# Three blocks of the first product in flight, and an even second product, in a mixture-of-experts loop

## What is computed

```python
a = jnp.einsum('th,eih->eti', hf, w1)
g = jnp.einsum('th,eih->eti', hf, w3)
eo = jnp.einsum('eti,ehi->eth', jax.nn.silu(a) * g, w2)
out = jnp.einsum('eth,te->th', eo, cw)
return hidden_states + out.reshape(B, S, H)
```

## Time and profile before

| | us |
|---|---|
| median of 3 runs (lowest to highest) | 2165.48 (2162.01 to 2167.72) |
| the profiled execution | 2174.44 |
| its span from first to last instruction | 2172.7 |
| TensorE matmul busy | 1881.4 |
| VectorE, ScalarE, GpSimd busy | 1453.2, 1220.9, 1219.0 |
| mean granted TensorE clock | 0.917 |

### The profile page before, as it was taken

How to read it: one execution, slowest core, us unless ns; L and a number is a source line. 1 busy time by engine, 2 the same in 40 slices (tenths; PEclk the granted TensorE clock), 3 DMA queues, 4 the chain that set the end, 5 groups by cost and what they waited for, 6 DMA issues and landing times. The chain is left out here.

```text
span 2172.7 us, 36357 instructions
## 1 busy us (share of the span) xinstructions
PE 1881.4 (87%) x12326; PEld 1352.7 (62%) x12326; DVE 1453.2 (67%) x2914; ACT 1220.9 (56%) x2305; POOL 1219.0 (56%) x989
## 2 busy tenths in 40 slices
PE   1898799999999999997994999925999999999996
PEld 0454355554454555553543988814889998899986
DVE  5477577777787877785762777844666666666663
ACT  0165566666666656674662554404666666666663
POOL 6443454545546445553324366642777777777775
PEclk8599899999999999997996999957999999999998
DMA  2655345555454566443503112126666666666662
GB/s 85 119 114 104 92 100 108 111 115 121 90 119 85 112 124 122 101 95 65 107 21 104 39 71 94 69 76 219 199 201 198 185 190 202 198 198 185 190 198 53
DMA packets 117005, 270.61 MB, mean 125 GB/s; under 512 B 15802, under 2 KB 49722, under 8 KB 116436
## 3 DMA queue, kind: packets, MB, share of 16 engines
q1 hardware_dynamic: 102516, 249.57, 43.5%
q0 software_dynamic: 14304, 18.72, 4.8%
HBM read 196.50 MB, written 71.73 MB: 123 GB/s over the span
## 5 line engine op out<-in xcount | busy, mean ns | idle before, releaser
L701 DVE TENSOR_REDUCE nraw<-ps 128x1 f32<-128x512 f32 x1024 | 649.2, 681 | 256.6 <-PE ps L848 254.8
L614 ACT ACTIVATE spare<-ps 128x512 f32<-128x512 f32 x1024 | 570.9, 602 | 394.7 <-PE ps L858 392.9
L1743 POOL TENSOR_TENSOR u_lo<-u_f,u_hi 128x256 fp32r<-128x256 f32 x273 | 343.6, 1268 | 164.6 <-ACT u_hi L1774 163.9
L1845 PE MATMUL ps_e<-x_hi,we_hi 128*128 128x256 f32 x1092 | 316.5, 290 | 9.0 <-DVE we_lo L1664 4.5
L848 PE MATMUL ps<-kst,qst 50*128 50x512 f32 x1024 | 290.8, 461 | 23.4 <-DVE nraw L701 17.2
L1845 PE MATMUL ps_e<-x_hi,we_lo 128*128 128x256 f32 x1092 | 305.5, 280 | 0.0
L1845 PE MATMUL ps_e<-x_lo,we_hi 128*128 128x256 f32 x1092 | 305.5, 280 | 0.0
L858 PEld LDWEIGHTS ps<-qst,kst 52*128 52x128 f32 x1024 | 106.6, 190 | 298.9 <-ACT spare L614 205.3
L858 PE MATMUL ps<-qst,kst 52*128 52x512 f32 x1024 | 281.8, 516 | 7.3 <-ACT spare L614 7.0
L870 PE MATMUL ps<-spare,vaug 128*32 128x512 f32 x2048 | 287.4, 635 | 0.0
L1704 DVE TENSOR_TENSOR u_f<-ps_e,silu 128x256 f32<-128x256 f32 x273 | 114.9, 421 | 235.2 <-PE ps_e L1845 133.9
(11 more groups left out here) (224 smaller groups left out, 3834.7 us busy)
## 6 DMA issues: line engine op xcount, KB each, us to landing
we_raw<-in_experts_w SPq DMA_DIRECT2D x117, 896.0 KB, 4.8
parts_kept<-parts SPq DMA_DIRECT2D x64, 512.0 KB, 3.3
kst<-parts_kept SPq DMA_DIRECT2D x192, 128.0 KB, 4.8
qst<-parts_kept SPq DMA_DIRECT2D x192, 128.0 KB, 7.2
x_raw<-xs SPq DMA_DIRECT2D x39, 259.0 KB, 2.8
x<-sum_tok SPq DMA_DIRECT2D x16, 512.0 KB, 2.6
x_tok<-x SPq DMA_DIRECT2D x16, 512.0 KB, 3.9
x_tok<-in_x SPq DMA_DIRECT2D x8, 512.0 KB, 4.5
```

The source lines that it names most:

```text
L614: act.activation(probs[:, e % 8], ps[:, score_bank(e, par)], ACT.Exp, scale=SCALE).then_inc(exp_made, 1)
L701: dve.tensor_reduce(nraw[:, g % 2, qt, half, i:i + 1], ps[:, max_bank(m, par)], AX.X, ALU.max, negate=True).then_inc(max_made, 1)
L1743: pool.tensor_tensor(u_lo[:, it], u_f[:, slot], u_hi[:, it].bitcast(F32), ALU.subtract).then_inc(ulo_made, 1)
L1845: ins = pe.matmul(ps[:, 2 * slot + c, 0:GR], left, right, start=m == 0, stop=m == len(terms) - 1)
```

## The change

- UPS = 3 slots for `silu` and `u_f`, and three PSUM banks for the first product: bank q % 3 for block q = 7n + it, with c = 0 in its first half and c = 1 in its second. `up` of q waits for `u_f` of q - 3, `u_f` of q for `u_lo` of q - 3. `silu` waits for both halves of its bank.
- LAG = 4: behind each `up` of block q stands `down` of block q - 4, the same in every place; four are left behind the loop.
- The sums of the second product have two pairs of banks by turns, and `eo_sb` two buffers: `put_out` waits for the adds of the step before the last, not the last.
- Both halves of the turned rows share bank 7. The turns stand in blocks 0 and 1, `x_hi` in blocks 1 and 3 and `x_lo` in block 4, both waiting for both turns. Before the loop both turns are issued without the wait for `x_lo` between them.
- `put_out` stands in block 5, the adds in block 5 (t = 0) and block 1 of the step after (t = 1). Behind the loop GpSimd issues the second add of step 37 and both of step 38.

```diff
@@ -60,6 +60,7 @@
 ROUTE_STEPS = 24
+UPS, LAG = 3, 4
 DX = D + 3
@@ -1607,11 +1608,11 @@
     x_lo = sb("x_lo", [P, 2, KD, GR], F32R)
-    silu = sb("silu", [P, 2, GR])
-    u_f = sb("u_f", [P, 2, GR])
+    silu = sb("silu", [P, UPS, GR])
+    u_f = sb("u_f", [P, UPS, GR])
     u_hi = sb("u_hi", [P, KI, GR], F32R)
     u_lo = sb("u_lo", [P, KI, GR], F32R)
-    eo = sb("eo_sb", [P, GT, D])
+    eo = sb("eo_sb", [P, 2, GT, D])
     x_in = [sem("x_in0"), sem("x_in1")]
@@ -1628,6 +1629,8 @@
     added = sem("added")
+
+    OUT_BANK, X_BANK = UPS, 7
 
@@ -1665,8 +1668,8 @@
             def lo_of_x(n, k, mt):
-                dve.wait_ge(xhi_made, n * 2 + mt + 1)
-                dve.scalar_tensor_tensor(x_lo[:, k, mt], ps[:, 7, 0:GR], rms_col[:, mt:mt + 1],
+                dve.wait_ge(xhi_made, n * 2 + 2)
+                dve.scalar_tensor_tensor(x_lo[:, k, mt], ps[:, X_BANK, mt * GR:(mt + 1) * GR], rms_col[:, mt:mt + 1],
                                          x_hi[:, k, mt].bitcast(F32), ALU.mult, ALU.subtract) \
@@ -1696,12 +1699,12 @@
                 for it in range(KI):
-                    slot = (k + it) % 2
-                    dve.wait_ge(silu_made, n * KI + it + 1)
-                    dve.wait_ge(up_mm, n * (2 * KI) + 2 * it + 2)
-                    if positive(n * KI + it - 1):
-                        dve.wait_ge(ulo_made, n * KI + it - 1)
-                    dve.tensor_tensor(u_f[:, slot], ps[:, 2 * slot + 1, 0:GR], silu[:, slot],
+                    q = n * KI + it
+                    dve.wait_ge(silu_made, q + 1)
+                    dve.wait_ge(up_mm, 2 * q + 2)
+                    if q >= UPS:
+                        dve.wait_ge(ulo_made, q - UPS + 1)
+                    dve.tensor_tensor(u_f[:, q % UPS], ps[:, q % UPS, GR:2 * GR], silu[:, q % UPS],
                                       ALU.mult).then_inc(u_made, 1)
@@ -1711,8 +1714,9 @@
                         lo_of_w(n + 1, 1 - k, it // 2)
-                    if it in (4, 6):
-                        lo_of_x(n + 1, 1 - k, (it - 4) // 2)
+                    if it == 4:
+                        for mt in range(KD):
+                            lo_of_x(n + 1, 1 - k, mt)
 
@@ -1731,23 +1735,26 @@
                 pool.indirect_dma_start(
-                    out=scratch["out"], in_=eo[:, t], in_offset=None,
+                    out=scratch["out"], in_=eo[:, n % 2, t], in_offset=None,
                     out_offset=bass.IndirectOffsetOnAxis(ap=targets[:, n % 3, t:t + 1], axis=0),
...
                 for it in range(KI):
-                    slot = (k + it) % 2
-                    pool.wait_ge(uhi_made, n * KI + it + 1)
-                    pool.tensor_tensor(u_lo[:, it], u_f[:, slot], u_hi[:, it].bitcast(F32),
+                    q = n * KI + it
+                    pool.wait_ge(uhi_made, q + 1)
+                    pool.tensor_tensor(u_lo[:, it], u_f[:, q % UPS], u_hi[:, it].bitcast(F32),
                                        ALU.subtract).then_inc(ulo_made, 1)
...
                         keep_rows(i, n, k)
-                    if n and it in (3, 6):
-                        add(n - 1, it // 6)
+                    if n >= 2 and it == 1:
+                        add(n - 2, 1)
+                    if n and it == 5:
+                        add(n - 1, 0)
 
             over_steps(pool, body)
+            add(STEPS - 2, 1)
             for t in range(GT):
@@ -1763,15 +1770,16 @@
             def hi_of_x(n, k, mt):
-                act.wait_ge(xt_mm, n * 2 + mt + 1)
-                act.activation(x_hi[:, k, mt], ps[:, 7, 0:GR], ACT.Copy, scale=rms_col[:, mt:mt + 1]) \
+                act.wait_ge(xt_mm, n * 2 + 2)
+                act.activation(x_hi[:, k, mt], ps[:, X_BANK, mt * GR:(mt + 1) * GR], ACT.Copy, scale=rms_col[:, mt:mt + 1]) \
                     .then_inc(xhi_made, 1)
...
                     act.wait_ge(down_kt, n * KI + it + 1 - KI)
-                act.activation(u_hi[:, it], u_f[:, (k + it) % 2], ACT.Copy).then_inc(uhi_made, 1)
+                act.activation(u_hi[:, it], u_f[:, (n * KI + it) % UPS], ACT.Copy) \
+                    .then_inc(uhi_made, 1)
 
@@ -1783,10 +1791,10 @@
                 act.wait_ge(share_made, n + 1)
-                if n:
-                    act.wait_ge(added, 16 * GT * n)
+                if n >= 2:
+                    act.wait_ge(added, 16 * GT * (n - 1))
                 for t in range(GT):
-                    act.activation(eo[:, t], ps[:, 4 + t, 0:D], ACT.Copy,
+                    act.activation(eo[:, k, t], ps[:, OUT_BANK + GT * k + t, 0:D], ACT.Copy,
                                    scale=shares[:, k, t:t + 1]).then_inc(eo_made, 1)
@@ -1797,22 +1805,22 @@
                 for it in range(KI):
-                    slot = (k + it) % 2
-                    act.wait_ge(up_mm, n * (2 * KI) + 2 * it + 1)
-                    if positive(n * KI + it - 1):
-                        act.wait_ge(u_made, n * KI + it - 1)
-                    act.activation(silu[:, slot], ps[:, 2 * slot, 0:GR], ACT.Silu) \
+                    q = n * KI + it
+                    act.wait_ge(up_mm, 2 * q + 2)
+                    if q >= UPS:
+                        act.wait_ge(u_made, q - UPS + 1)
+                    act.activation(silu[:, q % UPS], ps[:, q % UPS, 0:GR], ACT.Silu) \
                         .then_inc(silu_made, 1)
...
                         hi_of_u(n, k, it - 1)
-                    if it == 2 and n:
+                    if it == 5 and n:
                         put_out(n - 1, 1 - k)
...
                         hi_of_w(n + 1, 1 - k, it // 2)
-                    if it in (3, 6) and not last:
-                        hi_of_x(n + 1, 1 - k, it // 6)
+                    if it in (1, 3) and not last:
+                        hi_of_x(n + 1, 1 - k, it // 2)
                 hi_of_u(n, k, KI - 1)
@@ -1823,17 +1831,17 @@
                     pe.wait_ge(x_in[k], i * 16 + 16)
-                if positive(n * 2 + mt):
-                    pe.wait_ge(xlo_made, n * 2 + mt)
+                if n:
+                    pe.wait_ge(xlo_made, n * 2)
                 for t in range(GT):
-                    ins = pe.transpose(ps[:, 7, t * P:(t + 1) * P],
+                    ins = pe.transpose(ps[:, X_BANK, mt * GR + t * P:mt * GR + (t + 1) * P],
                                        x_raw[:, k, t, mt * P:(mt + 1) * P], ident[:, :])
...
             def up(n, k, it):
-                slot = (k + it) % 2
-                if positive(n * KI + it - 1):
-                    pe.wait_ge(u_made, n * KI + it - 1)
+                q = n * KI + it
+                if q >= UPS:
+                    pe.wait_ge(u_made, q - UPS + 1)
                 for c in range(2):
@@ -1842,15 +1850,15 @@
                     for m, (left, right) in enumerate(terms):
-                        ins = pe.matmul(ps[:, 2 * slot + c, 0:GR], left, right, start=m == 0,
+                        ins = pe.matmul(ps[:, q % UPS, c * GR:(c + 1) * GR], left, right, start=m == 0,
                                         stop=m == len(terms) - 1)
...
                     pe.wait_ge(wlo_made, n * 3 + 3)
-                    if positive(n):
-                        pe.wait_ge(eo_made, GT * n)
+                    if n >= 2:
+                        pe.wait_ge(eo_made, GT * (n - 1))
                 pe.wait_ge(ulo_made, n * KI + it + 1)
@@ -1858,7 +1866,7 @@
                     for m, (left, right) in enumerate(terms):
-                        ins = pe.matmul(ps[:, 4 + t, 0:D], left, right, start=it == 0 and m == 0,
+                        ins = pe.matmul(ps[:, OUT_BANK + GT * k + t, 0:D], left, right, start=it == 0 and m == 0,
                                         stop=it == KI - 1 and m == len(terms) - 1)
@@ -1870,17 +1878,14 @@
                     up(n, k, it)
-
-                    if it >= 3:
-                        down(n, k, it - 3)
-                    elif it < 2 and not (isinstance(n, int) and n == 0):
-                        down(n - 1, 1 - k, KI - 2 + it)
-                    if it in (2, 5) and not last:
-                        turn_rows(i + k, n + 1, 1 - k, it // 5)
-                down(n, k, KI - 3)
+                    q = n * KI + it - LAG
+                    if q >= 0:
+                        down(q // KI, q // KI % 2, q % KI)
+                    if it < KD and not last:
+                        turn_rows(i + k, n + 1, 1 - k, it)
 
             over_steps(pe, body)
-            for it in (KI - 2, KI - 1):
+            for it in range(KI - LAG, KI):
                 down(STEPS - 1, (STEPS - 1) % 2, it)
```

## The result

The changed kernel takes 2095.75 us in the median of 4 runs (2092.38 to 2096.51), the kernel before 2166.08 in the same session: ratio 0.9675, 95% interval 0.9658 to 0.9692, or 70 us less. Forecast were 2099 us and 66.5 us less.

A forecast was written before the change was run, and what follows sets the result against it. TensorE was taken as the bound, waiting 1.82 us of each 16.92 us step. Loop -69.0, start -1.2 and end +3.7 make -66.5 us; off the median of 2165.48 that gives 2099 us, likeliest case 2086 to 2111.

The forecast's parts named there:

- TensorE bounds, and idles 1.82 us a step: Experts' loop: TensorE has 15.10 us of work in a steady step of 16.92 us; the other 1.82 us is waiting.
- The loop: 592.0 us forecast: First to last up after the change: matmuls 567.5, transposes 17.5, low clock 2.0, filling 1.0, handoffs 4; 660.96 us before.
- The allowance of 0.1 us a step for handoffs: Added to TensorE's 15.10 us in each of the loop's 39 steps: 4 us in all.
- the 1 us for filling: Added to the loop's time for filling step 0: 1.0 us.
- Every link has 1.7 us or more to spare: In one changed step, each engine's result is ready at least 1.7 us before it is needed.
- The walk: One changed step laid out engine by engine from the end of up(0), with each result's ready time and need.
- 1.13 at down(4) and 0.7 elsewhere: Waiting in a step before the change: 1.13 us of stall ahead of down(4), 0.7 us in smaller pieces.
- The lock as rival: VectorE's we_lo shuts GpSimd out and sets the step: 11% for part of it (2111 to 2145 us), 3% for all.
- The clock as rival: TensorE's granted clock drops to half level in the loop; at 0.81 in the mean 2220 us, slower. Chance 3%.
- The start and the end: Start: no wait for x_lo between the turns, -1.2 us. End: four chained adds left, not three, +3.7 us.
- GpSimd near 85%: GpSimd's busy share in the changed loop, against 78 of 100 us before.

The follow-up runs named there:

- lag3: The changed kernel with LAG = 3 in place of 4: 2100.83 us, ratio 0.9684 to the kernel before.
- lag2: The changed kernel with LAG = 2 in place of 4: 2228.49 us, ratio 1.0282 to the kernel before.
- adds56: The changed kernel with both adds in one step, t=0 at block 5 and t=1 at block 6: 2153.08 us, ratio 0.9933 to the kernel before.
- xlo6: The changed kernel with the second x_lo back in block 6, behind the third we_lo: 2167.98 us, ratio 0.9993 to the kernel before.
- before_x: The kernel before with only the turns (blocks 0, 1; both halves in bank 7), x_hi (1, 3) and x_lo (4) changed: 2173.5 us, ratio 1.0020.
- ulo_twice2: The changed kernel with GpSimd computing u_lo a second time in blocks 4 and 6: 2107.23 us, ratio 0.9717 to the kernel before.
- before_add4: The kernel before with the first add moved from block 3 to block 4: 2301.48 us, ratio 1.0604.

## Why the prediction was right, point by point

- **TensorE bounds, and idles 1.82 us a step.** Right. 15.08 us a step in the mean against 15.10, and no wait of TensorE left in the steady loop. The pitch of the matmuls is unchanged.
- **The loop: 592.0 us forecast, 586.5 measured.** The pure work was 587.0. The allowance of 0.1 us a step for handoffs (4 us) and the 1 us for filling were not there: a wait whose semaphore has long been raised costs TensorE nothing that the trace shows. These two terms are why the loop came out 5.5 us shorter than forecast. The end took 0.8 us of that back and the start 0.2 us: 71.0 us less in the profile where 66.5 were forecast.
- **Every link has 1.7 us or more to spare.** The walk's times came true to 0.4 us where no lock was in doubt (u_lo(2) and u_lo(4) to 0.1, x_lo and u_f(6) 0.3 us earlier than forecast), and it took the later of two outcomes for blocks 5 and 6. The least to spare was 2.6 us, at u_lo(2). lag3 confirms the spare time: a whole block of distance could go. lag2 and adds56 mark its limits. What the walk did not hold was a place in a queue that has to wait: it took the add as 1.03 us of GpSimd's time, which is right only where the add before has landed (adds56).
- **What carries the gain.** The prediction listed lag and slots first, and did not say what each is worth. The runs do: three slots and the fourth block nothing; the second x_lo ahead of the third we_lo all of it (xlo6); the second add in the next step 56 us of it (adds56). These don't add up: each is a path of its own, and the step is as long as the longest, as before_x shows. The prediction split the 1.82 us into 1.13 at down(4) and 0.7 elsewhere. The sum was right, but the two are not separate limits, as the expectation of before_x took them to be. That an even order with a lag of three is needed is shown from one side only: lag 2 is too little. The old uneven order with the other parts changed wasn't run, and neither were the changed kernel with one eo_sb or with put_out in its old place.
- **The lock as rival.** It didn't come about, but is close: 1.5 us more a step on GpSimd and it begins to show (ulo_twice2). I had written against it that the add keeps its usual length beside other work, from the row at 1710.03 us. That reading failed: that add began 1.04 us ahead of we_lo. In before_add4, where it begins 0.22 us behind we_lo's start, it took 3.23 us. Counted among what the lock stretches, the add makes the rival likelier than I had it.
- **The clock as rival.** It didn't come about in the changed kernel, 1.00 throughout. before_add4 shows its condition: idle stretches of 3.4 us or so, once a step. The waits of 1.4 to 1.6 us in lag2 and xlo6 left the full clock.
- **The start and the end.** -1.2 forecast, -1.0 measured; +3.7 forecast, +4.5 measured. The first of the four adds comes 1.86 us behind the last up (forecast 1.65), and they are 4.5 to 4.7 us apart, not 4.4.
- **GpSimd near 85%.** Wrong: 80%. The row numbers' cast (L1729) is now 0.18 us, as it no longer falls under we_lo.

## What to carry to other kernels

Lay each engine's queue on one step's time axis and compare when each result is ready with when it is needed; that told before its run that one instruction's place would cost some 1.7 us a step (xlo6: 1.8), while the number of buffers told nothing. Where a wait ends a chain over several engines, look for the whole way round the loop: a part that shortens another path shows no gain by itself, and may still be worth everything once the longest is gone. An instruction that waits for a DMA to land belongs where it has long landed, since everything behind it in its queue waits too; and moving it without checking what it then falls beside can cost more than the stall that it cures.

## What the runs showed of the hardware

- The issue of the indirect, adding DMA on GpSimd is held up by VectorE's subtraction with two operands in SBUF: 3.2 us in place of 1.56 where it starts 0.2 us behind it (before_add4). It is held until the subtraction ends: in all traces here 186 adds start behind we_lo's start and with more than 0.12 us of it to come, and each ends 1.43 to 1.50 us behind we_lo's end. None of the others takes over 1.63 us, not even where we_lo starts within 0.3 us behind it. The Trainium skill (SBUF — State Buffer, "Who interferes with whom") infers that such a VectorE instruction takes only the read interface, and that descriptor generation needs the write interface, so it wouldn't be held. These adds are held; whether it is that step or the reading of their row numbers (`targets`, in SBUF) isn't shown.
- The lock works both ways: we_lo takes 2.01 us alone, but 2.29 us where GpSimd's u_lo began 0.3 us before it (kernel before, u_lo at 1701.57 and we_lo at 1701.89 us), and GpSimd's tiny cast went from 1.98 to 0.18 us by its place alone.
- In the changed kernel the adds take 5.5 us from issue to landing in the median, against 3.9 before and 3.9 in adds56. It is mostly the add in block 1: 5.0 to 7.4 us between 1718 and 2040 us, where that in block 5 takes 4.4 to 4.9 in most steps. The one at 2050.03 us, the same place in the last step, lands after 3.8 us, and by then no weights are loaded any more (DMA share 0.12 from 2050 to 2060 us, 0.70 before). So the loads beside it are the likely cause; no run isolates it.
- In before_add4 TensorE's matmuls start 0.21 us apart, the lower of the two levels (1.2 of 2.4 GHz), some 0.9 us after it resumed from 3.4 us of idle time; in xlo6, with 1.6 us of idle time once a step, they don't (granted clock 1.00 in 1700 to 1800 us).
